# Sorted edge records of eight edges instead of four, in a one-core graph layer on Trainium2

## The chip, the cores and the metric

One core of one Trainium2 chip runs the whole layer as one program. The metric is the time of an execution on the device in microseconds (us). The engines are TensorE (PE in the profile), VectorE (DVE), ScalarE (ACT), GpSimd (POOL) and SyncE (SP, which issues DMAs); each runs its own list of instructions and waits on semaphores.

## The reference

The input is `x` (6250 nodes x 256), 100,000 edges (`src`, `dst`, `edge_weight`) and weights. What is computed:

```python
xn = layernorm(x)
agg = segment_sum(xn[dst] * edge_weight[:, None], src, 6250)     # messages, summed by src
gnn = relu((xn + agg) @ W1 + b1) @ W2 + b2
# mix: per head (8 of 32), k = ln(xn_h), v = ln(xn_h), kv = k^T v / N; out = xn_h @ kv, plus xn
x = x + gnn + mix(xn)
# ffn: 16 experts, the best 2 of each node by its gate, weighted by a softmax, then layernorm
x = x + ffn(layernorm(x))
```

`src` is spread evenly over the nodes. The change lies in the part that computes `agg`.

## The kernel before

The nodes are 49 tiles of 128 (`NT`), and a tile of source nodes is a bucket. `agg` is made in two stages.

**The sort** (the first block, lines 505 to 1031). Edges lie 784 to a partition, and are treated as 28 groups (`NGRP`) of 28 columns, so 3584 edges a group. Each group is sorted by bucket. VectorE and TensorE count the edges of each bucket in each group, round each count up to whole records of `QE` = 4 edges, and sum these up to a place for every record ("quad" in the names) both in its group and in the whole sorted list. Then comes a loop over the 28 groups (7 rounds of 4, `GPR` = 4). In it VectorE's `matrices` (L891 to L924) builds one-hot matrices that say in which row and column each edge goes, `moving` and `row_hot`, and the addresses of the records, `quad_idx`; ScalarE's `weights` (L690) makes the half of `moving` that carries the weights, by 28 copies (L698); TensorE's `sort` (L640) sums 28 products into a bank of `NQ`\*`QW` = 64 rows of 128, and turns it, by way of ScalarE's `copy_quads` (L710, L714), so that a group lies as 128 partitions of `NQ` = 8 records. GpSimd's `scatter` (L597) writes it out: for each of the `NQ` records of a partition one indirect DMA (L603), 128 lanes of one record (4 edges x source code and weight, 32 bytes) to `rec_dram`. There are two buffers of `moving` and `row_hot`, and four of `quads` and `quad_idx`; VectorE (L922) and ScalarE (L713) wait for the scatters of four groups back before they write one again. ScalarE also computes LayerNorm tiles in this loop (`norm`, seven a round, in a share of three and one of four), and SP stores them. After the first four groups VectorE has `bucket_order` (L930), and after the last the tables of parts (L965 to L1030), which SP stores (L546 to L552) before the block ends.

**The gather** (the second block, from line 1122). The sorted list is cut into tiles of 128 edges, `TQ` = 128/`QE` records each; `ET` is their number at most, and two neighbours are a pair (`EP` = `ET`/2). GpSimd's `pair` (L1271) fetches for every tile the rows of `xn` by an indirect DMA of 128 lanes of 1 KB (L1276), in order, all `ET` of them. Twelve pairs fit (`PB`); a pair's place is released by SP (L1142) when TensorE is done with it. Where a pair holds edges of more than one bucket, it is used once for each: this gives `UT` parts at most. For each part VectorE builds two matrices 128x128 of weights at the places of the edges' source nodes (L1420), TensorE multiplies them with the rows (L1301, L1302), and VectorE adds the sum to the bucket's tile (L1437). Other work is woven in by the number of the part ("unit" u), written out by hand: seven groups of head statistics from unit `heads_from[g]`, the matrix `kv`, and from `slots_from` on the 49 node tiles, each turned, multiplied, normed and given to its experts at set distances after `turn_unit[s]`. `turn_unit[s]` is the later of `slots_from` + 1 + 14s/3 and `done_by[s + 1]` + 2, where `done_by[r]` is the part after which r buckets are sure to be done. So the node tiles start late, catch up, and then follow the buckets. GpSimd's gathers carry no such weave.

The blocks after it are the experts (from line 1667) and the final mixing and norm (from line 1940).

The sizes follow from `QE`, and all of this is fixed when the program is built: with `QE` = 4, 26,096 records at most, `ET` = 816, `EP` = 408, `UT` = 456. VectorE and TensorE read the numbers of parts in batches of `LB` = 6, so `UT` has to be a multiple of 6.

Of the kernel before, what the change touches and what calls it, by code (L numbers as in the profile page):

```python
# [22 lines left out]
ALU = mybir.AluOpType  # L23
# [4 lines left out]
P = 128  # L28
# [30 lines left out]
def gps_layer(nc, x, src, dst, edge_weight, gW1, gb1, gW2, gb2, klw, klb, vlw, vlb,  # L59
              gate_w, gate_b, w1, b1, w2, b2, gamma, beta, out):  # L60
    N, D = x.shape
    E = src.shape[0]
    H = gW1.shape[1]
    NX, _, F = w1.shape
    HD = D // HEADS
    DC = D // P
# [3 lines left out]
    NT = -(-N // P)  # L70
# [6 lines left out]
    GC, NGRP = 28, 28  # L77
    EC = GC * NGRP
    assert P * EC >= E > (P - 1) * EC
    QE = 4  # L80
    REC = 2
    QW = QE * REC

    NQ = -(-((GC * P + NT * (QE - 1)) // QE) // P)
    TQ = P // QE
    EFULL = E // EC
    EREST = E - EFULL * EC
    ROUND = 24

    ET = -(-(NGRP * ((GC * P + NT * (QE - 1)) // QE)) // (TQ * ROUND)) * ROUND  # L90
    EROUNDS = ET // ROUND


    EP = ET // 2
    TQ2 = 2 * TQ
    QUADS = NGRP * ((GC * P + NT * (QE - 1)) // QE)
    done_by = [0] + [((r + 1) * QUADS // NT - 1) // TQ2 + 1 + r for r in range(NT)]
    UT = done_by[NT]
    assert ET * TQ >= QUADS and UT <= EP + NT - 1
    BU = -(-UT // P)  # L100
    LB = 6
    ESEL = 28
    PB = ROUND // 2
    RB = -(-EP // P)
# [23 lines left out]
    with ctx:  # L128
        def sb(name, shape, dt=F32):
            return ctx.enter_context(nc.sbuf_tensor(name, shape, dt))  # L130

        def sem(name):
            return ctx.enter_context(nc.semaphore(name))
# [46 lines left out]
        row_hot = [a.rearrange("p (j r) -> p j r", j=GC) for a in row_hot]  # L180
        col_hot = [carve(GC * NQ * QE).rearrange("p (j c) -> p j c", j=GC) for _ in range(2)]
        moving = [carve(GC * NQ * QW) for _ in range(2)]
# [33 lines left out]
        quads_i = restart.bitcast(I32)  # L216
# [4 lines left out]
        pos_i, part_i = carve(EC).bitcast(I32), carve(EC).bitcast(I32)  # L221
# [7 lines left out]
        source = carve(ET).bitcast(I32)  # L229
        lane = carve(2 * UT)  # L230
        weight_s = carve(2 * UT)
        code_i = lane.bitcast(I32)
# [8 lines left out]
        tile_rows = nd[:, 0:BT * P * REC].rearrange("p (c s w) -> p c s w", c=BT, w=REC)  # L241
        part_from, part_end = [sq[:, h * UT:(h + 1) * UT] for h in range(2)], [sq[:, 2 * UT:3 * UT]]
        assert BT * P * REC <= GT * D and 3 * UT <= GT * D and 2 * BU * P * REC <= ESEL * P
        assert 4 * UT + ET + ROUND * D + ESEL * P <= slot_at
# [127 lines left out]
        tiles_i = sb("tiles_i", [P, NT], I32)  # L372
# [33 lines left out]
        s_dve = sem("dve_steps")  # L406
# [98 lines left out]
        with nc.Block() as block:  # L505
# [230 lines left out]
            def _(dve):  # L736
# [46 lines left out]
                    dve.tensor_scalar(quads_i[:, b0 * NGRP:(b0 + nb) * NGRP], bank[c][:, 0:nb * NGRP], float(QE - 1), None,  # L783
                                      ALU.add).then_inc(s_dve, 1)
                dve.wait_ge(s_dve, n.add(len(BANKS)))
                dve.tensor_scalar(quads_i, quads_i, 2, None, ALU.arith_shift_right).then_inc(s_dve, 1)
                assert QE == 1 << 2
                dve.wait_ge(s_dve, n.add())
                dve.tensor_copy(quads_bg, quads_i).then_inc(s_dve, 1)
                dve.tensor_copy(gb(quads_gb), bg(quads_i).rearrange("p b g -> p g b")).then_inc(s_dve, 1)  # L790
# [80 lines left out]

                dve.tensor_tensor(pos_i, pos, rank, ALU.add).then_inc(s_dve, 1)
                dve.wait_ge(s_dve, n.add())
                dve.tensor_scalar(part_i, pos_i, 2, P - 1, ALU.arith_shift_right, ALU.bitwise_and).then_inc(s_dve, 1)
                dve.wait_ge(s_dve, n.add())
                dve.tensor_copy(row_f, part_i).then_inc(s_dve, 1)
                dve.wait_ge(s_dve, n.add())
                dve.tensor_scalar(part_i, pos_i, QE - 1, None, ALU.bitwise_and).then_inc(s_dve, 1)
                dve.tensor_scalar(pos_i, pos_i, 9, None, ALU.arith_shift_right).then_inc(s_dve, 1)
                dve.wait_ge(s_dve, n.add(2))  # L880
                dve.scalar_tensor_tensor(col_f, pos_i, float(QE), part_i, ALU.mult, ALU.add).then_inc(s_dve, 1)
                dve.wait_ge(s_dve, n.add())
# [82 lines left out]
                def then(ins):  # L965

                    ins.then_inc(s_dve, 1)
                    dve.wait_ge(s_dve, n.add())

                in_pairs = lambda: dve.tensor_scalar(tiles_i[:], tiles_i[:], 6, None, ALU.arith_shift_right)  # L970
                assert TQ2 == 1 << 6
                then(dve.tensor_scalar(tiles_i[:], tiles_f[:], -1.0, None, ALU.add))
                then(in_pairs())
                then(dve.tensor_copy(off[:, 0:NT], tiles_i[:]))
# [118 lines left out]
        BC = len(CHUNKS)  # L1093
        assert len(TILES) == BT <= 7 and BC == 8 and UT % LB == 0
        chunk_at = lambda c, h, n: slice(h * UT + c * P, h * UT + c * P + n)
# [26 lines left out]
        with nc.Block() as block:  # L1122
            @block.sync
            def _(sp):
# [17 lines left out]
                def release(r, q):  # L1142
                    _, done = nc.values_load_multi_w_load_instructions(
                        release_row[0:1, ds(r * PB + q, 1)], engines=(nc.sync.engine,), min_val=1, max_val=UT,
                        skip_runtime_bounds_check_because="a count of parts: one at least of each pair")
                    sp.wait_ge(s_sum, done[0])
                    sp.sem_inc(s_go, 1)
# [137 lines left out]
            def _(pe):  # L1285
                packed = []

                def unit(u):
                    if u % LB == 0:
                        _, loaded = nc.values_load_multi_w_load_instructions(  # L1290
                            place_row[0:1, u:u + LB], engines=(nc.tensor.engine,), min_val=32, max_val=16 * ET + 15,
                            skip_runtime_bounds_check_because="a pair's number and its place, both limited")
                        packed[:] = loaded
                    pe.wait_ge(s_landed, packed[u % LB] >> 4)
                    pe.wait_ge(s_sel, 2 * u + 2)
                    if u >= SUMB:
                        pe.wait_ge(s_acc, u + 1 - SUMB)
                    place = nc.s_assert_within(packed[u % LB] & 15, 0, PB - 1,
                                               skip_runtime_bounds_check_because="a remainder of PB")
                    at = place * (2 * D)  # L1300
                    pe.matmul(sums_at(u), edge_sel[:, 2 * u % ESEL, :], rows_flat[:, ds(at, D)], start=True, stop=False)  # L1301
                    pe.matmul(sums_at(u), edge_sel[:, (2 * u + 1) % ESEL, :], rows_flat[:, ds(at + D, D)],  # L1302
                              start=False, stop=True).then_inc(s_sum, 1)
# [110 lines left out]
            def _(dve):  # L1414
# [10 lines left out]
                def unit(u):  # L1425
                    if u % LB == 0:
                        _, loaded = nc.values_load_multi_w_load_instructions(
                            bucket_row[0:1, u:u + LB], engines=(nc.vector.engine,), min_val=0, max_val=NT - 1,
                            skip_runtime_bounds_check_because="a number of a bucket")
                        buckets[:] = loaded  # L1430
                    if u + LEAD < UT:
                        build(u + LEAD)
                    dve.wait_ge(s_sum, u + 1)
                    if u:
                        dve.wait_ge(s_acc, u)
                    at = ds(buckets[u % LB] * D, D)
                    dve.tensor_tensor(xh[:, at], xh[:, at], sums_at(u), ALU.add).then_inc(s_acc, 1)  # L1437
# [634 lines left out]
```

## Time and profile before

| | |
|---|---|
| runs shown | 2440.65 us median of 3 (2439.96 to 2444.09) |
| the profiled execution | 2446.2 us, its span from first to last instruction 2444.5 us |
| busy, share of the span | PE 67%, DVE 59%, ACT 30%, POOL 59% |
| first scatter starts, last ends | 230.5 us, 609.4 us |
| first gather starts, last ends | 625.9 us, 1741.7 us |
| mean granted TensorE clock | 0.822 of full |

A busy share is a mean over stages with different limits, so the stages are read one by one: by windows of the trace, by what an engine waited for ahead of a group of instructions, and by single instructions in order of time. "Issue" is time in which an engine waited for nothing that the profile shows. The busy time of an indirect DMA on POOL is the time in which GpSimd writes its descriptors; the landing is later and is given apart.

### The profile page before, as it was taken

What the parts mean: (1) busy time and instruction counts of PE and PEld (TensorE: products, weight loads), DVE (VectorE), ACT (ScalarE), POOL (GpSimd) and SP (SyncE); (2) the same over time, 40 slices, a digit from 0 to 9 for tenths busy, and PEclk for the clock granted to TensorE, in tenths of its full rate; (3) what the DMA queues carried; (4) which work ended last, traced back from release to release, by engine and by line L of the source; (5) the groups of instructions that cost most, each with busy time, mean ns of one, the idle gap of its engine ahead of it and who ended that gap; (6) DMA issues with size and microseconds to landing.
All of it is one profiled execution on the core that took longest, in us unless ns stands there. A gap on an engine that the chain in (4) does not pass through costs nothing. (4 is left out here: it accounts for less than half of the span.)

```text
span 2444.5 us, 39839 instructions
## 1 busy us (share of the span) xinstructions
PE 1639.3 (67%) x9188; PEld 1403.0 (57%) x9189; DVE 1443.0 (59%) x4105; ACT 739.3 (30%) x2173; POOL 1453.5 (59%) x1576
## 2 busy tenths in 40 slices
PE   5603666662355587877777777877648999999800
PEld 2203665662244476666666666666547888888700
DVE  8499756553676666665666656656443343334379
ACT  4804655551000014342222222222222333333200
POOL 8002888887777677566777777777314555555400
PEclk9856877776677799997888888888779999999955
DMA  4000000004443234333444444444464111111274
GB/s 148 0 0 16 18 18 17 28 22 3 152 130 109 86 115 139 114 118 99 123 124 127 122 123 124 125 123 124 73 212 137 62 61 60 58 60 62 52 274 155
DMA packets 134728, 226.98 MB, mean 93 GB/s; under 512 B 33383, under 2 KB 87967, under 8 KB 134606
## 3 DMA queue, kind: packets, MB, share of 16 engines
q0 software_dynamic: 57664, 138.89, 20.4%
q1 hardware_dynamic: 49246, 60.85, 8.2%
q10 hardware_dynamic: 27696, 25.83, 3.3%
q8 instruction: 50, 0.82, 0.1%
q14 instruction: 72, 0.59, 0.1%
HBM read 183.09 MB, written 42.38 MB: 92 GB/s over the span
## 5 line engine op out<-in xcount | busy, mean ns | idle before, releaser
L1276 POOL DMA_INDIRECT lower<-xn_rows,lower x816 | 817.1, 1001 | 299.1 <-issue 224.1
L603 POOL DMA_INDIRECT edge_records_sorted<-lower x224 | 310.9, 1388 | 233.2 <-ACT lower L714 165.3
L1437 DVE TENSOR_TENSOR xh<-xh,bank 128x256 f32 x456 | 189.4, 415 | 269.0 <-PE bank L1302 268.1
L1301 PE MATMUL bank<-lower 128*128 x912 | 313.6, 429 | 28.7 <-SPq L1152 12.5
L1420 DVE TENSOR_SCALAR lower<-iota_n,lower 128x128 f32<-128x128 f32 x912 | 279.9, 355 | 65.8 <-issue 49.0
L647 PE MATMUL bank<-lower 128*64 128x128 f32 x1568 | 227.9, 319 | 123.6 <-ACT lower L698 120.8
L1302 PE MATMUL bank<-lower 128*128 x912 | 302.9, 417 | 0.0
L647 PEld LDWEIGHTS bank<-lower 128*64 128x64 f32 x1568 | 221.7, 167 | 128.2 <-DVE lower L913 121.4
L1832 POOL DMA_INDIRECT expert_rows<-arena,dest_idx x114 | 114.7, 1006 | 215.0 <-DVE arena L1927 199.0
L1918 DVE TENSOR_SCALAR arena<-bank,b_tile 128x128 f32<-128x128 f32 x456 | 128.4, 344 | 175.7 <-PE bank L1861 175.7
L1861 PEld LDWEIGHTS bank<-arena 128*128 128x128 f32 x1824 | 223.5, 193 | 5.9
L1882 PE MATMUL bank<-upper,arena 128*128 x912 | 226.4, 391 | 0.1
L1861 PE MATMUL bank<-arena 128*128 128x128 f32 x1824 | 223.9, 276 | 0.0
L1302 PEld LDWEIGHTS bank<-lower 128*128 128x128 f32 x912 | 194.2, 213 | 32.9
L698 ACT ACTIVATE lower<-lower 128x32 f32<-128x32 f32 x784 | 169.3, 309 | 123.8 <-DVE lower L898 123.7
L1301 PEld LDWEIGHTS bank<-lower 128*128 128x128 f32 x912 | 175.4, 214 | 52.7 <-issue 38.4
L1882 PEld LDWEIGHTS bank<-upper,arena 128*128 128x128 f32 x912 | 165.6, 191 | 30.3 <-issue 4.3
L1899 ACT ACTIVATE arena<-lower 128x1024 f32 x114 | 120.5, 1057 | 59.9 <-issue 59.6
L1927 DVE COPY arena<-bank 128x256 f32<-128x256 f32 x114 | 48.4, 425 | 146.2 <-PE bank L1882 146.2
L1840 POOL DMA_INDIRECT arena<-xn_rows,tok_idx x114 | 109.5, 960 | 38.3 <-issue 31.5
L1905 ACT ACTIVATE arena<-bank 128x256 f32<-128x256 f32 x114 | 43.8, 384 | 289.6 <-PE bank L1871 289.6
L1331 PE MATMUL bank<-ident,lower 128*128 128x128 f32 x98 | 27.9, 381 | 122.1 <-ACT lower L1196 116.5
(316 smaller groups left out, 2558.4 us busy)
## 6 DMA issues: line engine op xcount, KB each, us to landing
lower<-xn_rows,lower POOLq DMA_INDIRECT x816, 2.8
lower<-in_L_ffn_w SPq DMA_DIRECT2D x16, 512.0 KB, 9.8
upper<-in_L_ffn_w SPq DMA_DIRECT2D x16, 512.0 KB, 10.7
xn_rows<-xh SPq DMA_DIRECT2D x7, 896.0 KB, 4.1
arena<-xn_rows ACTq DMA_DIRECT2D x7, 896.0 KB, 5.4
lower<-xn_rows ACTq DMA_DIRECT2D x49, 128.0 KB
xn_rows<-lower ACTq DMA_DIRECT2D x49, 128.0 KB
x_plus_beta<-lower ACTq DMA_DIRECT2D x49, 128.0 KB
```

What stands on the lines that cost most here:

```text
L603: pool.indirect_dma_start(rec_dram, bass.IndirectOffsetOnAxis(quad_idx[i][:, c:c + 1], 0), quads[i][:, c * QW:(c + 1) * QW], None).then_in ...
L647: mm = pe.matmul(bank[6 + p][0:NQ * QW, 0:P], moving[p][:, e].rearrange("p c w -> p (c w)"), row_hot[p][:, e, :], start=e == 0, stop=e == ...
L698: done = act.activation(moving[p][:, e, :, 1], col_hot[p][:, e, :], ACT.Copy, scale=group_wgt[p][:, e:e + 1])
L1276: pool.indirect_dma_start(edge_rows[:, t % ROUND, :], None, xn_dram, bass.IndirectOffsetOnAxis(source.bitcast(U32)[:, t:t + 1], 0)).then_i ...
L1301: pe.matmul(sums_at(u), edge_sel[:, 2 * u % ESEL, :], rows_flat[:, ds(at, D)], start=True, stop=False)
L1302: pe.matmul(sums_at(u), edge_sel[:, (2 * u + 1) % ESEL, :], rows_flat[:, ds(at + D, D)], start=False, stop=True).then_inc(s_sum, 1)
L1420: dve.tensor_scalar(edge_sel[:, (2 * u + h) % ESEL, :], iota_n[:], lane[:, at:at + 1], weight_s[:, at:at + 1], ALU.is_equal, ALU.mult).the ...
L1437: dve.tensor_tensor(xh[:, at], xh[:, at], sums_at(u), ALU.add).then_inc(s_acc, 1)
L1861: mm = pe.matmul(bank[2 + p][:, m * P:(m + 1) * P], w1_tile[p][:, c * F + m * P:c * F + (m + 1) * P], tokT[p][:, c * P:(c + 1) * P], start ...
L1882: mm = pe.matmul(bank[6 + p][:, 0:D], hidT[p][:, m * P:(m + 1) * P], upper[:, ds(e * (FC * D) + m * D, D)], start=False, stop=m == FC - 1)
L1899: act.activation(w1_tile[p], lower[:, ds(e * (DC * F), DC * F)], ACT.Copy).then_inc(s_w1t, 1)
L1918: dve.tensor_scalar(hidT[p][:, m * P:(m + 1) * P], bank[2 + p][:, m * P:(m + 1) * P], b1_tile[:, ds(t + m * XT, 1)], 0.0, ALU.add, ALU.max ...
```

## The change

A record holds eight edges instead of four (`QE`, and with it the shifts that divide by it). A group has `NQ` = 4 records a partition for 8, and a record is 64 bytes (`QW` = 16 words for 8); the product `NQ`\*`QW` stays 64 and `NQ`\*`QE` stays 32. `TQ` goes from 32 to 16 records a tile of 128 edges, whose bytes stay. Rounding up each bucket of each group to eight edges makes the list longer: at most 13,720 records of eight, so `ET` = 864, `EP` = 432. `done_by[NT]` would be 477 and is rounded up to 480, which is `UT`. The number of chunks in which the records of the parts are loaded (`BC` = 8) stays, and so does the number of tiles of source numbers (`BT` = 7). `slots_from` goes from 83 to 87, `heads_from` from 9, 18, 27, 37, 46, 55, 65 to 9, 19, 29, 38, 48, 58, 68, and the last node tile's turn from unit 458 to 482.

```diff
-    QE = 4
+    QE = 8
+    QSHIFT = 3
+    assert QE == 1 << QSHIFT
...
+    LB = 6
+    done_by[NT] = -(-done_by[NT] // LB) * LB
     UT = done_by[NT]
-    assert ET * TQ >= QUADS and UT <= EP + NT - 1
+    assert ET * TQ >= QUADS and UT < EP + NT - 1 + LB
     BU = -(-UT // P)
-    LB = 6
...
-                dve.tensor_scalar(quads_i, quads_i, 2, None, ALU.arith_shift_right).then_inc(s_dve, 1)
-                assert QE == 1 << 2
+                dve.tensor_scalar(quads_i, quads_i, QSHIFT, None, ALU.arith_shift_right).then_inc(s_dve, 1)
...
-                dve.tensor_scalar(part_i, pos_i, 2, P - 1, ALU.arith_shift_right, ALU.bitwise_and).then_inc(s_dve, 1)
+                dve.tensor_scalar(part_i, pos_i, QSHIFT, P - 1, ALU.arith_shift_right, ALU.bitwise_and).then_inc(s_dve, 1)
...
-                dve.tensor_scalar(pos_i, pos_i, 9, None, ALU.arith_shift_right).then_inc(s_dve, 1)
+                dve.tensor_scalar(pos_i, pos_i, QSHIFT + 7, None, ALU.arith_shift_right).then_inc(s_dve, 1)
...
-                in_pairs = lambda: dve.tensor_scalar(tiles_i[:], tiles_i[:], 6, None, ALU.arith_shift_right)
-                assert TQ2 == 1 << 6
+                in_pairs = lambda: dve.tensor_scalar(tiles_i[:], tiles_i[:], 5, None, ALU.arith_shift_right)
+                assert TQ2 == 1 << 5
```

## Rows read from the trace of the kernel before

**Rows 1.** Groups by line on GpSimd: busy, mean ns | idle before, what ended it
```profile
L1276 POOL DMA_INDIRECT lower<-xn_rows,lower x816 | 817.1, 1001 | 299.1 <-issue 224.1 <-SPq L1147 75.0
L603 POOL DMA_INDIRECT edge_records_sorted<-lower x224 | 310.9, 1388 | 233.2 <-ACT lower L714 165.3 <-issue 68.0
```
**Rows 2.** The scatter's line: durations in ns, who waited for it, landing
```profile
L603 POOL DMA_INDIRECT edge_records_sorted<-lower x224: 963/968/3987, 230.5 to 608.4; - x112
...
  DVE lower L923: 125.8, 23
...
DMA to landing us min/median/max: 2.1/2.1/15.1
```
**Rows 3.** Window of the sort: busy us (instructions) by engine, PEclk, DMA share, GB/s
```profile
228.50:569.90 341.40, 223.32 (x1507) 213.85 (x1507) 208.59 (x217) 195.38 (x854) 280.89 (x193) 0.77 0.08 21
```
**Rows 4.** The gather's line: two windows of it, its durations and landing
```profile
625.80:1140.00 514.20, 360.47 (x341) 0.83 0.38 116
1140.00:1741.70 601.70, 456.58 (x476) 0.84 0.44 123
...
L1276 POOL DMA_INDIRECT lower<-xn_rows,lower x816: 947/953/2729, 625.9 to 1740.7; - x164
...
DMA to landing us min/median/max: 2.7/2.8/6.9
```
**Rows 5.** The line that centres a group of heads, seven times
```profile
L1456 DVE TENSOR_TENSOR lower<-arena x7: 2024/2026/2026, 667.3 to 844.0; 128x1792 f32<-128x1792 f32 x7
```
**Rows 6.** Order of time, 261 to 269 us: start, duration, engine, line
```profile
261.01 1.70 POOL L603 DMA_INDIRECT edge_records_sorted<-lower  x1 [0.30 <-issue]
...
263.77 3.88 DVE L913 TENSOR_TENSOR lower<-upper,iota_n 128x3584 f32<-128x3584 bf16 x1
264.51 3.98 POOL L603 DMA_INDIRECT edge_records_sorted<-lower  x1 [0.30 <-issue]
...
268.80 0.97 POOL L603 DMA_INDIRECT edge_records_sorted<-lower  x1 [0.30 <-issue]
```
**Rows 7.** Order of time, 221 to 255 us, ScalarE and TensorE
```profile
221.19 6.05 ACT L698 ACTIVATE lower<-lower 128x32 f32<-128x32 f32 x28 [0.15 <-DVE lower L898]
...
228.64 0.27 ACT L710 ACTIVATE lower<-bank 64x128 f32<-64x128 f32 x1 [1.41 <-PE bank L647]
...
229.23 6.33 PE L647 MATMUL bank<-lower 128*64 128x128 f32 x56
...
229.46 2.06 ACT L704 ACTIVATE xh<-upper,arena 128x256 f32<-128x256 f32 x4
...
237.63 0.25 ACT L710 ACTIVATE lower<-bank 64x128 f32<-64x128 f32 x1
...
238.20 8.00 PE L647 MATMUL bank<-lower 128*64 128x128 f32 x56
...
246.23 0.27 ACT L710 ACTIVATE lower<-bank 64x128 f32<-64x128 f32 x1 [1.50 <-PE bank L647]
...
254.19 2.02 ACT L698 ACTIVATE lower<-lower 128x32 f32<-128x32 f32 x9 [6.77 <-DVE lower L898]
```
**Rows 8.** VectorE: a step over 400 elements, and one over 200
```profile
L900 DVE TENSOR_TENSOR lower<-iota_pc,upper 128x400 f32<-128x400 f32 x25 | 14.2, 569 | 0.0
...
582.12 0.37 DVE L1028 TENSOR_TENSOR lower<-lower,arena 128x200 f32<-128x200 f32 x1
```
**Rows 9.** Order of time at the end of the sort
```profile
569.90 0.17 DVE L923 CAST lower<-lower 128x8 uint32<-128x8 f32 x1 [5.21 <-DMA edge_records_sorted<-lower]
...
586.34 0.51 SPq L551 DMA_DIRECT2D tile_pair_parts<-tiles_i  x1
...
615.08 0.36 SPq L1127 DMA_DIRECT2D lower<-edge_records_sorted  x1
```
**Rows 10.** Window in the later gather: PE, PEld, DVE, ACT, POOL, PEclk, DMA
```profile
1200.00:1300.00 100.00, 77.98 (x381) 66.43 (x379) 62.94 (x242) 25.30 (x72) 75.91 (x80) 0.86 0.42 124
```

## The prediction

> **What bounds the kernel now.** I began with the costliest groups of the page: two groups of indirect DMAs hold most of GpSimd's time, the gather at L1276 and the scatter at L603 [rows 1]. The reader is to see the idle time beside them: for the scatter one wait of 165.3 us, and else nothing but "issue", 68.0 us over 223 gaps, 0.30 each. So GpSimd runs without a pause from the first scatter at 230.5 us to the last, which starts at 608.4 and ends at 609.4 [rows 1, 2]. The view of L603 says who waits for it: VectorE, 125.8 us in all, at L923 (the slot of four groups back must have landed) [rows 2]. So in this stretch, "the sort", GpSimd sets the pace: 28 groups in 378.9 us (310.9 busy + 68.0 issue), 13.5 us a group, while the DMA engines are busy 0.08 of the time [rows 3].
>
> The gather starts at 625.9 and ends at 1741.7 us. From 1140 on it issues 476 in 601.7 us, 1.264 us each; before that 341 in 514.2 us, 1.508 each [rows 4]. There GpSimd waits for places to come free (75 us in all, "SPq L1147") [rows 1], first behind head statistics that come every 29.5 us ((844.0-667.3)/6) for some nine parts each [rows 5], then behind the node tiles catching up. What comes after 1742 us has no instruction in the diff.
>
> **The change part by part.** The constants first. A record of 8 instead of 4 edges: NQ 8 to 4, QW 8 to 16, so NQ\*QW stays 64 and the one-hot columns NQ\*QE stay 32; TQ 32 to 16; UT 456 to 480 parts, EP 408 to 432 pairs, ET 816 to 864 gathers. The matmuls, ScalarE's copies and VectorE's three large products of the sort keep their shapes.
>
> *Scatters, 224 to 112.* An undisturbed one takes 0.968 us and 0.304 us of issue (68.0/224). 224 x 1.272 = 284.9 us; the stretch is 378.9, so 94.0 us are something else. The timeline shows it: a scatter that starts while VectorE runs a product of two SBUF operands ends 0.84 us after it. L913 runs 263.77 to 267.65, the scatter of 264.51 ends at 268.49 [rows 6]. This loss belongs to VectorE's groups and not to the number of scatters: 94.0/28 = 3.36 us a group on average, and at most what 261.01 to 268.80 shows, 7.79 us for three scatters, 3.97 lost. With the scatters halved GpSimd alone would need 112 x 1.272 = 142.5 us + 94.0 = 236.5, or with the larger loss 142.5 + 111.2 = 253.7.
>
> The Trainium skill ("SBUF — State Buffer", Who interferes with whom) says that a VectorE instruction with two SBUF inputs and a GpSimd instruction that reads SBUF share a port pair, held for the whole instruction by whichever came first. By that rule the loss stays with VectorE's instructions, and the sum would be the 253.7 above; by the opposite reading, a loss for each scatter, it would be 142.5 + 47 = 189.5. The trace bears out the rule.
>
> Does a scatter's price change with 64 bytes per lane instead of 32? The gather issues 1 KB per lane and its shortest is 947 ns, the 32-byte scatter's 963 [rows 2, 4]. I cost it at nothing; if each cost 0.2 us more (as between its median 968 and the 1.18 of a lightly blocked one), 22 us.
>
> *What is late next in the sort.* The ring of four hides VectorE from GpSimd; once GpSimd is faster, the loop ScalarE to TensorE sets the pace. The rows at the start, before the ring filled, show it bare [rows 7]: ScalarE reads the sums of a group at 228.64, 237.63 and 246.23, periods of 8.99 (with four LayerNorm tiles, 2.06 us, in it) and 8.60. The second is TensorE's: its matmuls took 6.33 us where they followed closely on the ones before, and 8.00 after 2.6 us (235.56 to 238.20) with only a transposition in it. A period without LayerNorm tiles and with short matmuls: 6.05 (28 copies) + 0.82 (229.46-228.64) + about 0.24 = 7.1 us. One round of four is then about 9.0 + 8.6 + 7.1 + 8.6 = 33.3, 8.3 each. VectorE needs less: in the window of 228.5 to 569.9 us, which holds 25 of its groups and `bucket_order`, it is busy 208.6 us [rows 3], so at most 8.3 a group, and three steps over 400 elements (0.57 us each) become 200 (0.37 at L1028) [rows 8]: 7.7. I take 8.5 (8.3 plus the coupling of three nearly equal loops), 27 x 8.5 = 229.5, + 6.8 us in which ScalarE waits for `bucket_order` [rows 7], + the last group's transposition and four scatters, 6: 242. Above GpSimd's 236.5 and below its 253.7, so they push one another: I take 245. Ends: 236.5 and, if every period is 9.2 (matmuls of 8.0 us and more throughout, LayerNorm or not), 27 x 9.2 + 12.8 = 261. The sort gains 378.9 - 245 = **134 us (118 to 142)**.
>
> *The end of the sort.* After its last group VectorE computes the part tables, 569.9 to 583.2, and SP stores them till 587 [rows 9]; now GpSimd's backlog until 609.4 covers this 17 us. With the new ring GpSimd has four groups of four scatters left, 16 x 1.272 = 20.4 us. It still covers the 17 plus the 2 that a store takes to land, with about 1 us to spare; if that cover is gone it costs 1 to 4 us. The barrier (609.4 to 615.1) stays.
>
> *Gathers, 816 to 864.* 48 x 1.264 = **60.7 us**, at the rate of the saturated part. Four of the 24 new parts, with three or four pairs, come before the node tiles start (slots_from 83 to 87). There VectorE's chain of head statistics sets the pace and extra units may fit in its gaps: 3.5 x 2 x 1.264 = 9 us less, so 52 at the low end. If all were issued at the slow part's 1.508, 72. I take 60: the catch-up ends at nearly the same unit (160, now 158), and past it the gathers run at the issue limit, which a lighter load per unit does not speed up. TensorE and VectorE get 24 more parts, 5% more of that work, in a stretch where they have 22% and 37% idle [rows 10]: hidden.
>
> *The rest.* `zeros` grows by 96 elements and the tables from 912 to 960 columns: under 0.3 us. The last tile's turn stays two units behind the last part (458 for 456, 482 for 480), so the tail after the last gather stays.
>
> Sum: -134 + 60 = -74. Against the profiled run: 2446.2 (span 2444.5 and 1.7 around it) - 74 = 2372; that run lies 5.5 above the median of the runs shown, 2440.65, so the forecast is 2440.65 - 74 = **2367 us**.
>
> **Rivals.**
> 1. *TensorE stays cold in the sort.* For: its granted clock there is 0.77 on average, and the matmuls after a wait took 8.00 us against 6.33 [rows 3, 7]. Against: the waits that cool it are mostly GpSimd's, and they go. With 9.5 us a period: 27 x 9.5 + 12.8 = 269, a gain of 110, less 60: 2391.
> 2. *GpSimd stays the bound and is blocked in every group as much as at 261 to 268.* For: VectorE's instructions, 208.6 us of 341.4 now [rows 3], will fill most of an 8.5 us period. Each scatter may wait: four in 10.4 us (3 in 7.79) [rows 6], 28 x 10.4 = 291, a gain of 88, less 60: 2413. Against: once GpSimd is behind, VectorE waits at L923 and the port comes free, which gives 9.06 a group, 253.7.
> 3. *The gather's landings become late and the kernel slower.* An empty place in a record reads row 0. There are 864 x 128 - 100,000 = 10,592 empty places for 4,448 now, so 12 of a gather's 128 lanes instead of 5 ask one row. If that makes landings late enough that GpSimd waits for places all through, as it does in the first part, 864 x 1.508 = 1303 us for 1115.9: +187 - 134 = +53, 2494. It decides against the change from a mean of (1115.9+134)/864 = 1.447 us a gather. Against: a landing takes 2.8 us in the median and 6.9 at worst, with twelve pairs of places to cover it, and the DMA engines are busy 0.44 [rows 4].
>
> That the scatters are not on the path is excluded by rows 2; that the record grows dearer than 0.2 us by the gather's price.
>
> **How the numbers follow.** Forecast (sort gain 118 to 142, gather +52 to +72) 74%; rival 1 12%, rival 2 6%, rival 3 4%; the remaining 4% for a mishap that eats most of the gain, half of it inside 0.2%. Faster by over 0.2% (about what a measurement of this kernel can tell): 0.93; within: 0.02; slower: 0.05. The forecast's own ends are -142 + 52 = -90 and -118 + 72 = -46, 2351 to 2395. The range takes both, and rival 1's 2391 is inside: 2348 to 2396.
>
> **What the changed profile would show.** L603 x112 with a median near 0.97 us and now with idle time other than "issue"; first to last scatter near 245 us; the wait of VectorE L923 on the scatters all but gone; ScalarE's L710 every 8.3 to 9 us; L1276 x864 at 1.26 us in its second part and a stage of about 1176 us; the barrier within 6 us of the last scatter. The forecast is wrong if the sort's period is over 9.5, or if scatters of 64 bytes take clearly longer than 0.97 us, or if "SPq L1147" grows much past 75 us.

## The result, and the profile after

Timed beside each other, four runs each: 2440.31 us before (2435.59 to 2444.09), 2380.35 us after (2379.05 to 2382.37), a ratio of 0.9756 with the interval 0.9737 to 0.9775. The change saves 60 us; the forecast was 2367, 74 us under the 2440.65 it started from, with a range of 2348 to 2396. The profiled execution has a span of 2379.1 us against 2444.5, 65.4 less.

The span was cut at points that both kernels have: the start of the first scatter, the end of the last scatter, the start of GpSimd's first load of the records (the second block's first work for it), the start of the first gather, the end of the last gather, and the first IOTA of the block after it. What each stretch took, in us:

```
stretch                                       before    after   change
start of the span to the first scatter         230.5    229.8     -0.7
first scatter to the end of the last           378.9    241.5   -137.4
from there to the first load of a record         6.4     30.6    +24.2
that load to the first gather                   10.1     10.1     +0.1
first gather to the end of the last           1115.8   1175.2    +59.4
from there to the next block (the tail)         43.8     32.4    -11.4
all the rest, from the IOTA to the end                            +0.5
```

Groups by line on GpSimd, after; they answer to [rows 1].

```profile
L1278 POOL DMA_INDIRECT lower<-xn_rows,lower x864 | 865.0, 1001 | 310.5 <-issue 239.3 <-SPq L1149 71.2
L606 POOL DMA_INDIRECT edge_records_sorted<-lower x112 | 200.8, 1793 | 205.1 <-ACT lower L717 174.9 <-issue 29.0 <-DVE lower L925 1.2
```

The scatter's line after, durations in ns, then who waited for it and its landing; it answers to [rows 2].

```profile
L606 POOL DMA_INDIRECT edge_records_sorted<-lower x112: 963/1126/4448, 229.8 to 470.3; - x112
...
  DVE lower L925: 4.7, 2
...
DMA to landing us min/median/max: 2.1/2.6/6.4
```

VectorE waited 125.8 us for scatters in the kernel before and waits 4.7 now. The shortest scatter still takes 963 ns, with records of 64 bytes. The median has gone up from 968 to 1126 ns: the time lost to VectorE is nearly the same (worked out below), and half as many scatters share it.

The window of the sort after, busy us and instructions of PE, PEld, DVE, ACT and POOL, then PEclk, DMA share and GB/s; it answers to [rows 3].

```profile
228.50:470.00 241.50, 188.91 (x1540) 179.98 (x1540) 206.30 (x266) 196.17 (x855) 199.81 (x111) 0.93 0.12 31
```

No engine of the four idles much in this window: they are busy for 189 to 206 of 241.5 us. TensorE's granted clock is 0.93 of 2.4 GHz here, against 0.77 in the same stretch before, where it had to wait for GpSimd.

Two windows of the gather's line after, and its durations; they answer to [rows 4].

```profile
512.00:1040.00 528.00, 382.79 (x362) 0.84 0.40 118
1040.00:1687.20 647.20, 482.19 (x503) 0.86 0.47 120
...
L1278 POOL DMA_INDIRECT lower<-xn_rows,lower x864: 947/953/2811, 512.0 to 1686.2; - x173
```

The second part issues 503 gathers in 647.2 us, 1.287 us each (1.264 before).

### The profile page after: what moved, and what is told of

The parts are those of the page before. It is cut to its first block and busy times, and to the rows that moved or that the text cites. A ratio compares the mean times of both kernels' runs of the same rounds, so it can differ in the third digit from the quotient of the medians.

```text
span 2379.1 us, 40341 instructions
## 1 busy us (share of the span) xinstructions
PE 1638.3 (69%) x9284; PEld 1371.2 (58%) x9285; DVE 1453.1 (61%) x4177; ACT 739.9 (31%) x2173; POOL 1391.3 (58%) x1512
## 5 line engine op out<-in xcount | busy, mean ns | idle before, releaser
L1278 POOL DMA_INDIRECT lower<-xn_rows,lower x864 | 865.0, 1001 | 310.5 <-issue 239.3
L1303 PE MATMUL bank<-lower 128*128 x960 | 342.9, 443 | 145.4 <-SPq L1154 121.3
L1439 DVE TENSOR_TENSOR xh<-xh,bank 128x256 f32 x480 | 199.7, 416 | 285.9 <-PE bank L1304 285.1
L1422 DVE TENSOR_SCALAR lower<-iota_n,lower 128x128 f32<-128x128 f32 x960 | 294.4, 357 | 69.7 <-issue 56.2
L606 POOL DMA_INDIRECT edge_records_sorted<-lower x112 | 200.8, 1793 | 205.1 <-ACT lower L717 174.9
L1304 PE MATMUL bank<-lower 128*128 x960 | 320.5, 419 | 0.0
L1303 PEld LDWEIGHTS bank<-lower 128*128 128x128 f32 x960 | 177.7, 213 | 212.1 <-issue 200.0
L650 PE MATMUL bank<-lower 128*64 128x128 f32 x1568 | 189.8, 285 | 125.1 <-ACT lower L701 120.8
L650 PEld LDWEIGHTS bank<-lower 128*64 128x64 f32 x1568 | 183.6, 145 | 128.8 <-DVE lower L915 121.4
L1304 PEld LDWEIGHTS bank<-lower 128*128 128x128 f32 x960 | 206.1, 215 | 35.1
L1216 ACT ACTIVATE std<-mv,eps_col 128x1 f32<-128x1 f32 x49 | 14.4, 295 | 320.1 <-DVE mv L1589 319.0
```

The source lines that it names most:

```text
L606: pool.indirect_dma_start(rec_dram, bass.IndirectOffsetOnAxis(quad_idx[i][:, c:c + 1], 0), quads[i][:, c * QW:(c + 1) * QW], None).then_in ...
L650: mm = pe.matmul(bank[6 + p][0:NQ * QW, 0:P], moving[p][:, e].rearrange("p c w -> p (c w)"), row_hot[p][:, e, :], start=e == 0, stop=e == ...
L1278: pool.indirect_dma_start(edge_rows[:, t % ROUND, :], None, xn_dram, bass.IndirectOffsetOnAxis(source.bitcast(U32)[:, t:t + 1], 0)).then_i ...
L1422: dve.tensor_scalar(edge_sel[:, (2 * u + h) % ESEL, :], iota_n[:], lane[:, at:at + 1], weight_s[:, at:at + 1], ALU.is_equal, ALU.mult).the ...
```

## The experiments

They ran in three groups, each group on a chip of its own, and to judge by the times none of these was the chip of the first timing. On them both kernels take 9 to 10% longer, most of it in the gather; the ratio of the two is the same. So a time is compared with the kernel before of its own group only: 2668.99 us (first), 2671.22 (second), 2684.68 (third).

```
kernel                   us       ratio, interval           scatters  gap to load  gathers  tail
first group
 half records, x224      2700.62  1.0105 (1.0075-1.0136)     362.6      12.8       1390.2   35.2
 capacity alone          2723.13  1.020  (1.017 -1.023 )     387.6       5.0       1386.8   34.8
 tables in rows          2592.46  0.9722 (0.9694-0.975 )     244.2      21.4       1387.0   37.6
 same, kernel before     2667.93  0.9999 (0.998 -1.0018)     385.9       5.0       1319.8   54.2
second group
 changed, again          2607.03  0.9757 (0.9723-0.9791)     244.0      31.1       1394.4   33.4
 half the scatters       2596.54  0.9726 (0.9694-0.9758)     237.5      23.5       1389.9   37.8
 tables early            2595.50  0.9729 (0.9702-0.9756)     263.4      11.5       1386.0   32.8
 early and in rows       2586.93  0.9683 (0.9657-0.9709)     255.9      11.5       1381.1   39.6
third group
 last turn later         2680.27  0.9993 (0.9978-1.0007)     387.6       5.0       1335.4   49.3
 changed, third time     2614.75  0.9749 (0.9725-0.9773)     251.5      24.5       1388.5   34.1
 tables in rows, again   2600.04  0.9682 (0.9658-0.9705)     253.3      15.3       1394.0   39.0
```

The last four columns are us from one profiled execution each, cut as above. Single executions differ: the changed kernel has 241.5, 244.0 and 251.5 us in the column of scatters, and 30.6, 31.1 and 24.5 in that of the gap. The sum of the two differs less, 272.1, 275.1 and 276.0. In what follows "..." marks lines of an edit that are left out.

**Half records: the new layout and capacity with 224 scatters of half a record each.** Is it the count of the scatters that gains?

```diff
     for c in range(NQ):
-        pool.indirect_dma_start(rec_dram, bass.IndirectOffsetOnAxis(quad_idx[i][:, c:c + 1], 0),
-                                quads[i][:, c * QW:(c + 1) * QW], None).then_inc(s_scat[i], 16)
+        for h in range(2):
+            pool.indirect_dma_start(rec_dram.rearrange("r (h w) -> (r h) w", h=2),
+                                    bass.IndirectOffsetOnAxis(quad_idx[i][:, 2 * c + h:2 * c + h + 1], 0),
+                                    quads[i][:, c * QW + h * QW // 2:c * QW + (h + 1) * QW // 2],
+                                    None).then_inc(s_scat[i], 16)
...
```

> The changed kernel, but each 64-byte record is scattered as two halves of 32 bytes, so a group has eight scatters again (224 in all) with all sizes, capacities and products of the change kept (VectorE gets two small steps more a group, some 0.3 us). Theory 'number of scatters': the first-to-last-scatter stretch goes back from 241 us to about 379 us (365 to 390), and since GpSimd then has a backlog that covers the stores of the tables, the gap from the last scatter to the next block falls from 30 to 6 us; the kernel loses 137 - 24 = 113 us, about 2493. Rival 'record layout' (the shorter steps over 200 elements and TensorE's warmer clock made the gain): the stretch stays within 20 us of 241 and the time within 20 us of 2380.

Measured: 1.0105, slower than the kernel before. GpSimd's groups of this kernel, as above:

```profile
L1286 POOL DMA_INDIRECT lower<-xn_rows,lower x864 | 859.1, 994 | 531.3 <-SPq L1157 288.1 <-issue 241.3 <-remote 1.8
L608 POOL DMA_INDIRECT edge_records_sorted<-lower x224 | 294.6, 1315 | 232.7 <-ACT lower L721 164.7 <-issue 68.0
```

With the count back at 224, "issue" is at 68.0 us again and the sort's stretch at 362.6. That is 2.4 us below what was expected (365 to 390), and the gain is gone; the loss against the changed kernel is some 93 us (0.0348 of 2670) where 113 was expected. The bytes and the layout are those of the changed kernel, so it is the number of scatters that set the pace before.

**Capacity alone: the kernel before with 864 gathers and 27,440 records of four.**

```diff
-    ET = -(-(NGRP * ((GC * P + NT * (QE - 1)) // QE)) // (TQ * ROUND)) * ROUND
+    ET = 864
...
-    QUADS = NGRP * ((GC * P + NT * (QE - 1)) // QE)
+    QUADS = 27440
...
+    LB = 6
+    done_by[NT] = -(-done_by[NT] // LB) * LB
...
```

> The kernel before with records of four edges, but with the capacity and the unit schedule of the change: 864 gathers, 480 parts, the last part rounded up, the same done_by. Theory: sort unchanged (379 us), the gather's first-to-last issue grows by 59 us (from 1116 to 1175), and the tail between the last gather and the next block shrinks from 44 to about 32 us, because the last two node tiles stand 13 units apart instead of 9: +48 us, about 2488. Rival 'the tail belongs to the sort or to chance': the tail stays 44 us and the time is 2440 + 59 = 2500. Rival 'more empty places slow the gathers': not testable by this one alone, but the rate of the second part would be over 1.264 us a gather.

Measured: 1.020, some 53 us. The gather takes 67.0 us more than in the kernel before with its tables in rows, on the same chip (1386.8 against 1319.8), and 51.4 more than in the last kernel with 816 gathers, "last turn later" of the third group; the tail is 19 and 15 us shorter than in these two. From these two runs and the repetition the change can be split: the capacity costs 53 us (0.020 of 2669.0), the layout gains 25 (1.0105 - 1.020) and the lower count 93 (0.9757 - 1.0105, on the kernels before of two groups); together -65, a ratio of 0.9757. By the intervals of the two ratios the 25 may be 9 to 41.

**Half the scatters: the changed kernel with two of the four records of each lane sent.** This kernel leaves out half of the records. Who sets the pace of the new sort?

```diff
-    for c in range(NQ):
+    for c in range(NQ // 2):
...
-        pool.wait_ge(s_scat[i], 16 * NQ * NG)
+        pool.wait_ge(s_scat[i], 8 * NQ * NG)
...
```

> The changed kernel with only two of the four scatters of each group (half of the records are never written, so the output lacks their edges); all products, copies and waits stay. Theory 'GpSimd, slowed by VectorE's port, still sets the sort's pace at 8.6 us a group': the stretch falls from 241 us to the pace of ScalarE and TensorE, 8.3 us a group or less, 225 to 232 us. Rival 'ScalarE and TensorE set it already': within 3 us of 241. Rival 'GpSimd alone sets it by a wide margin': under 215 us.

Measured: the stretch is 237.5 us, against 244.0 for the changed kernel of the same group. GpSimd's group:

```profile
L606 POOL DMA_INDIRECT edge_records_sorted<-lower x56 | 134.5, 2401 | 268.4 <-ACT lower L717 259.9 <-issue 8.5
```

Against the changed kernel of the same group GpSimd is spared 93 us (203.8 - 134.5 busy, 31.8 - 8.5 issue), and the stretch 6.5. That is no more than the stretch of the changed kernel itself differs from run to run (241.5 to 251.5). ScalarE reads the sums of the groups in the same four periods over and over, 9.18, 8.74, 7.43 and 8.71 us, which are also those of the changed kernel in its first profile (9.18, 8.74, 7.42, 8.71), with twice the scatters. In the profile of its own group the changed kernel has rounds with 10.0 and 8.7 in the place of 8.74 and 7.42; whether GpSimd has a part in those is not shown, and the 6.5 us are the most that it can be. For the rest the loop of ScalarE and TensorE sets the pace. That the stretch would fall to 225 to 232 was wrong.

**Tables in rows.** In the part tables entry u = c * 128 + p lies in partition p, column c. Neighbours in a partition are 128 entries apart in DRAM, so they are stored in pieces of 4 bytes. Here partition p holds entries 4p to 4p+3, so a piece is 16 bytes.

```diff
-    sp.dma_start(to.rearrange("(c p) -> p c", p=P), a).then_inc(s_bkst, 16)
+    sp.dma_start(to.rearrange("(p c) -> p c", p=P), a).then_inc(s_bkst, 16)
...
-    units = iota_pc[:, 0:BU]
+    units = iota_u[:]
...
```

> The changed kernel, with the parts numbered p*4+c instead of c*128+p on the partitions while the tables are made, so that each of the seven table stores at the end of the sort writes 128 pieces of 16 bytes instead of 512 of 4; the sorting, the gathers and the schedule are unchanged. Theory 'the stores of single words are the path': the stores land in a third of the time (landing 16 us to about 5, the wait for them 21 us to 6 to 9), the last scatter's landing no longer stands behind them, and the next block starts 12 to 17 us after the last scatter instead of 30: 13 to 18 us faster, 2362 to 2367. Rival 'the barrier and the queue of GpSimd are slow in themselves' (its drain took 9.2 us for 2.7 before): less than 5 us gained.

Measured: SP's wait for the stores is 10.7 us, the gap 21.4 against 30.6 in the first profile of the changed kernel. Both are better, and neither is as good as expected (6 to 9, and 12 to 17).

SP's waits in this kernel, 460 to 500 us: who waited for whom, us in total, times, longest.

```profile
SPq L509 <- DMA tile_pair_parts<-tiles_i: 10.7, 1, 10.7
SPq L509 <- PEq L509: 9.3, 1, 9.3
```

The same edit in the kernel before, where GpSimd's backlog should cover the stores:

> The same renumbering of the parts in the kernel before. Theory 'the backlog of scatters covered the stores': there it is worth nothing, within 3 us of 2440, though the stores land as early as in the changed kernel with the same edit. Rival 'the stores cost the same in both kernels': 13 to 18 us faster here too.

Measured: 0.9999, although SP's wait became shorter there too (21.4 us in the first trace of before):

```profile
SPq L506 <- PEq L506: 13.1, 1, 13.1
SPq L506 <- DMA tile_pair_parts<-tiles_i: 9.1, 1, 9.1
```

So the stores cost nothing before and cost time after: the change took away the work of GpSimd that lay over them.

**The changed kernel again, in the second group.**

> The changed kernel itself once more, so that the kernels of this call have it beside them on the same chip. Ratio to the kernel before 0.975; sort 241 us from first to last scatter, gap to the next block 30 us.

0.9757 beside 0.9756 of the first timing.

**Tables early: the part tables are computed and stored before the last round of the sort** (they need the counts only, and the counts are known).

```diff
-    with dve.Fori(2, NG) as r:
+    with dve.Fori(2, NG - 1) as r:
...
+    part_tables()
+    rounds(NG - 1)
```

> The changed kernel with the tables of parts computed by VectorE before the last round of four groups instead of after it, so that their stores go out while scatters are still being written. Theory 'the stores (21 us from issue to the last landing) are what the change uncovered at the sort's end': the gap from the last scatter to the next block falls from 30 to 6 to 13 us; VectorE's 13 us are hidden by the ring of four as long as GpSimd is behind, so the stretch grows by 0 to 8 us: 10 to 24 us faster than the changed kernel, ratio to before about 0.967. Rival 'VectorE has no slack in the sort': the stretch grows by the whole 13 us and only about 8 are gained. Rival 'GpSimd's drain of 9.2 us at the block's end is a price of its own': the gap stays above 13.

Measured: 0.9729. That is 11.5 us under the changed kernel of the group by the medians, but the intervals overlap (0.9702 to 0.9756, 0.9723 to 0.9791), so no gain is shown. The gap falls from 31.1 to 11.5 us, and the sort's stretch grows from 244.0 to 263.4: their sum was 275.1 and is 274.9. VectorE's 13 us of table steps have no slack in the sort, as the rival has it; why the stretch grew by more than 13 is not shown. The gap shows what the stores did. The scatter's line and the end of GpSimd's wait for their landing, in this kernel:

```profile
L606 POOL DMA_INDIRECT edge_records_sorted<-lower x112: 965/1040/4584, 230.3 to 492.7; - x112
...
L508 POOLq COMPARE_BRANCH  x1: 38/38/38, 494.9 to 494.9; - x1
```

The last scatter starts at 492.7 and ends a microsecond later, and the wait ends 1.2 us after that. Most of the gap that is left is a DRAIN of 9.2 us (below).

**Early and in rows: both.**

> Both: the tables before the last round and the stores in pieces of 16 bytes. Theory: the stores are hidden already, so it is like e7_tables_early within 3 us, or a little faster if the stores of single words delayed landings of scatters that VectorE waits for. Rival 'store pieces cost wherever they stand': 5 us or more faster than e7_tables_early.

0.9683, below the interval of the changed kernel. It is 8.6 us faster than tables early, so the rival (5 or more) fits and "within 3 us" does not; but the intervals of the two overlap a little, and where short pieces cost time in it is not shown: the gap is 11.5 us in both.

**Last turn later: the kernel before with the last node tile's turn at unit 461 for 458**, for the tail, which had become 11.4 us shorter.

```diff
+    turn_unit[NT - 1] += 3
```

> The kernel before with one number changed: the last node tile's turn stands at unit 461 instead of 458, so that it comes 12 units after the one before it, as in the changed kernel (13), and not 9. Theory 'the shorter tail comes from this order': the time between the last gather and the next block shrinks by 10 to 20 us (to 33 to 35 us), and the kernel is that much faster, ratio about 0.994. Rival 'the tail shrank by the lighter load per unit or by chance': the tail stays at 44 to 54 us.

Measured: 0.9993 where 0.994 was expected, and a tail of 49.3 us. The place of the last turn isn't the cause of the short tail.

**The changed kernel a third time, and its tables in rows again**, on one chip.

> The changed kernel beside the next one. Ratio 0.975; gap at the sort's end 31 us, of which 9.2 us are GpSimd's drain.

> e3_tables_in_rows once more, in one call with the changed kernel, as the version that may beat both. Gap 21 us, gather starting 9 us earlier than in the changed kernel, 9 us faster than it, ratio to before 0.972. Rival: the difference does not stand out of the noise, which on these chips is 0.3%.

0.9749 and 0.9682; the intervals (0.9725 to 0.9773, 0.9658 to 0.9705) do not overlap. Tables in rows is the best simple version: 14.7 us, 0.6%, under the changed kernel, and 3.2% under the kernel before. The gap accounts for 9.2 us of it (15.3 against 24.5). The rest the profiles don't place: in the profiled executions the gather and the tail are 5.5 and 4.9 us longer with the tables in rows, and the two profiled times (2604.13 and 2599.18) do not show the gain of the medians.

## Why the prediction was right, and where it was not

**The sort: -134 (118 to 142) forecast, -137.4 measured.** The reasoning held in its parts. Order of time after, 336 to 362 us, ScalarE's reads of a group's sums and TensorE's matmuls between them:

```profile
336.00 0.25 ACT L713 ACTIVATE lower<-bank 64x128 f32<-64x128 f32 x1
336.74 6.30 PE L650 MATMUL bank<-lower 128*64 128x128 f32 x56
...
345.18 0.25 ACT L713 ACTIVATE lower<-bank 64x128 f32<-64x128 f32 x1
345.92 7.96 PE L650 MATMUL bank<-lower 128*64 128x128 f32 x56
...
353.92 0.27 ACT L713 ACTIVATE lower<-bank 64x128 f32<-64x128 f32 x1 [1.65 <-PE bank L650]
354.71 6.30 PE L650 MATMUL bank<-lower 128*64 128x128 f32 x56
...
361.34 0.25 ACT L713 ACTIVATE lower<-bank 64x128 f32<-64x128 f32 x1
```

The periods are 9.18, 8.74 and 7.42, and 8.71 to the next at 370.05: a round of four of 34.05 us, 8.5 a group. The forecast had 9.0, 8.6, 7.1 and 8.6, 8.3 on average, from the few groups at the start of the old stretch [rows 7]; the 0.2 added for the coupling was a guess, and a good one. Both lengths of the matmuls, 6.3 us where they follow closely and 8.0 after a wait, came back too.

**The loss to VectorE stays with VectorE's instructions.** Before it was 94.0 us for 224 scatters. After, it is 200.8 - 112 x 0.968 = 92.4; with 56 scatters 134.5 - 56 x 0.968 = 80.3; with 224 of the new layout 294.6 - 224 x 0.968 = 77.8. A loss for each scatter would have been 47 us after, and 23.5 with 56 scatters. One of the blocked scatters, after:

```profile
344.54 3.88 DVE L915 TENSOR_TENSOR lower<-upper,iota_n 128x3584 f32<-128x3584 f32 x1
345.49 3.78 POOL L606 DMA_INDIRECT edge_records_sorted<-lower  x1 [0.30 <-issue]
```

It ends at 349.27, 0.85 us after VectorE's 348.42. The Trainium skill ("SBUF — State Buffer", Who interferes with whom) has the port pair held for a whole instruction by whichever came first; the traces agree, 92.4 us beside 94.0 at half the count.

**The end of the sort is the term that was mis-sized: nothing to 4 us forecast, 24.2 measured.** This is the step of the prediction that was wrong. It said that four groups of scatters, 20.4 us, are left, and "It still covers the 17 plus the 2 that a store takes to land". No row showed 2 us for a store; it is what a scatter takes [rows 2]. The tables' stores consist of 3584 single words of 4 bytes, and the view of the line of six of the seven has, after, from issue to landing:

```profile
DMA to landing us min/median/max: 9.9/15.3/16.7
```

The seventh, issued last, took 21.4 us. The median of the six was 17.0 before as well, and cost nothing: GpSimd was busy with its scatters until then. That row was not among those read for the prediction. The order of time after shows the last scatters issued among the stores (SPq is the queue of SP's own):

```profile
466.49 0.96 POOL L606 DMA_INDIRECT edge_records_sorted<-lower  x1 [0.30 <-issue]
466.69 0.38 SPq L553 DMA_DIRECT2D tile_pair_parts<-tile_bucket_i  x1
...
469.87 0.51 SPq L554 DMA_DIRECT2D tile_pair_parts<-tiles_i  x1
470.31 0.97 POOL L606 DMA_INDIRECT edge_records_sorted<-lower  x1 [0.30 <-issue]
...
501.86 0.99 POOL L1269 DMA_INDIRECT lower<-edge_records_sorted,tiles_i  x1 [30.59 <-POOLq L508]
```

SP's wait there:

```profile
SPq L508 <- DMA tile_pair_parts<-tiles_i: 20.9, 1, 20.9
```

The last scatter ends at 471.3 us. The instructions that close the block, after, with their durations in ns and their start:

```profile
L508 SPq COMPARE_BRANCH  x1: 38/38/38, 491.3 to 491.3; - x1
...
L508 POOLq COMPARE_BRANCH  x1: 38/38/38, 491.6 to 491.6; - x1
L508 POOLq DRAIN  x1: 9218/9218/9218, 491.7 to 491.7; - x1
```

and before:

```profile
L505 POOLq COMPARE_BRANCH  x1: 38/38/38, 612.0 to 612.0; - x1
L505 POOLq DRAIN  x1: 2685/2685/2685, 612.2 to 612.2; - x1
```

Before, GpSimd's wait for its scatters to land was over 2.6 us after the last one ended (609.4 to 612.0), now 20.3 us after (471.3 to 491.6), in the same moment as SP's wait for the stores. The queues' traffic from 476 to 480 us, after: q1 carries the stores, q0 what GpSimd issued; packets, MB, share of 16 engines.

```profile
q1 hardware_dynamic: 700, 0.00, 167.5%
q0 software_dynamic: 34, 0.01, 32.6%
```

Five to nine us after the last scatter ended, packets of scatters are still under way among the stores' single words. (The landing in the view of the scatter's line after, 6.4 us at most, doesn't show this; nor is it seen why both waits last 6 us longer than the last packet, before 485.)

The kernel before shows the same, and rows 2 had a sign of it, the 15.1 us at the end of the scatters' landings. Its stores are issued from 583.2 us on. The scatter's line before, for the scatters up to 583.0 us and for the six after them, with their landings:

```profile
L603 POOL DMA_INDIRECT edge_records_sorted<-lower x204: 963/968/3987, 230.5 to 583.0; - x102
DMA to landing us min/median/max: 2.1/2.1/5.1
...
L603 POOL DMA_INDIRECT edge_records_sorted<-lower x6: 966/967/970, 583.0 to 589.3; - x6
DMA to landing us min/median/max: 15.1/15.1/15.1
```

So scatters that are issued beside the stores are no cover for them: they are held up with them. Before it did no harm, since the last scatter came 22 us after the last store was issued. That makes 17.7 of the 24.2 us. The other 6.5 are the DRAIN, 9.2 us for 2.7.

The runs bear out the first part. From the first store issued to the end of GpSimd's wait the changed kernel takes 24.9, 24.6 and 25.7 us in its three profiles, though its last scatter ended 20.3, 20.8 and 14.3 us before that end. With pieces of 16 bytes it is 14.9 and 16.4 us. With the stores ahead of the last round GpSimd's wait ends 1.2 us after the last scatter; and in the kernel before the shorter stores gain nothing. The DRAIN no run explains. The prediction had named the sign, a barrier within 6 us of the last scatter; the next block's first work came 30.6 us after it.

**Gathers: +60 forecast, +59.4 measured.** 503 in the second part took 1.287 us each for 1.264, and the slow first part became shorter: 362 in 528.0, 1.459 for 1.508. Errors of a few us in each direction, and the total right; that they cancelled is luck.

**The tail: unchanged forecast, -11.4 measured.** "The last tile's turn stays two units behind the last part (458 for 456, 482 for 480), so the tail after the last gather stays" was wrong. The first instruction of the last turn on TensorE, and the first of the next block, before:

```profile
1762.32 0.66 PE L1331 MATMUL bank<-ident,lower 128*128 128x128 f32 x2 [5.91 <-ACT lower L1196]
...
1785.51 0.24 POOL L1698 IOTA lower<- 128x114 f32 x1 [43.83 <-POOLq L1122]
```

and after:

```profile
1699.48 0.41 PE L1333 MATMUL bank<-ident,lower 128*128 128x128 f32 x2 [0.90 <-ACT lower L1198]
...
1719.57 0.24 POOL L1700 IOTA lower<- 128x114 f32 x1 [32.38 <-POOLq L1124]
```

Before, the turn starts 20.6 us after the last gather (1741.7) and TensorE has idled 5.91 us for it; after, 12.3 us (1687.2) and 0.90. The capacity alone brings the short tail as well (34.8 us against 54.2). All profiles with 864 gathers have 32 to 40 us there and all with 816 have 44 to 54, so it goes with the capacity and its schedule of 480 units. Moving the turn did not bring it; what in the schedule does is open.

**The sum.** Forecast -134 + 60 = -74. Measured -137.4 + 24.2 + 59.4 - 11.4 - 0.2 = -65.4 between the profiled executions, -60 between the medians. Without the short tail, which nothing in the prediction foresaw, it would have been -54. Two unforeseen terms of opposite sign kept the error small, and that is luck, though -54 too would have been inside the range.

**The rivals.** TensorE cold in the sort: its clock rose to 0.93 and a group took 8.5 us, no. GpSimd blocked in every group, 291 us: 241.5, no. Late landings from row 0: the shortest gather stays at 947 ns, and the wait for places is 71.2 us for 75.0, no. The layout's gain of 25 us with an unchanged number of scatters had no term of its own: In the profiles the stretch of the scatters is 25.0 us shorter with half records than with the capacity alone (362.6 against 387.6), and 17.8 of these are a shorter busy time of GpSimd (294.6 against 312.4), so a smaller loss to VectorE. That this comes from VectorE's steps over 200 elements instead of 400 is likely and not shown.

## What to carry to other kernels

When a bound engine is relieved, list what ended within its backlog, and look up the landing of each DMA there by its own line: a duration of issue says nothing of it, and a store of 512 single words took 10 to 21 us here where a scatter took 2. A backlog that shares the DMA engines with the stores it should cover may be held up by them. And the groups at the start of a pipelined stretch, before its ring has filled, show the period of the next bound: read there, 8.3 us a group was forecast and 8.5 measured.

## What the runs showed of the hardware that was not expected

GpSimd's DRAIN at the end of the sort's block took 2685 ns in each of the five profiles with 224 scatters and 9218 ns in each of the seven with 112; with 56 it took 4645. It was the same whether GpSimd had waited 1.2 us for the landing or 20.3. The lines, of half the scatters and of the tables in rows (third group):

```profile
L508 POOLq DRAIN  x1: 4645/4645/4645, 486.1 to 486.1; - x1
```

```profile
L509 POOLq DRAIN  x1: 9218/9218/9218, 488.8 to 488.8; - x1
```

It costs 6.5 us at one place, and its cause is open.

A second thing: to judge by the times four chips ran these kernels, and one was 9 to 10% faster than the three others. The difference lies in the gather, 1175.2 us against 1388.5 for the same kernel, with the same duration of the single gather. Its line in the changed kernel's third run:

```profile
L1278 POOL DMA_INDIRECT lower<-xn_rows,lower x864: 947/953/2722, 517.5 to 1905.1; - x173
...
  SPq L1149: 286.1, 137
```

GpSimd waits 286.1 us for places to come free there, 71.2 on the first chip. What makes them late was not found; it is no matter of the change, since kernels with 816 gathers wait 285.6 and 301.5 us on these chips. The ratio of the two kernels was the same on the three chips that ran both, 0.9749 to 0.9757, so a forecast in us is worth less across chips than one in per cent.
